# ScalarE takes its PSUM-emptying steps one tile place earlier in a transformer block on one core

## What is computed

```python
x = x + 0.5 * ffn(layernorm(x), Wq, Wk, Wv, Wo, Wff)
x = x + attn(layernorm(x), w_qkv, b_qkv, w_o, b_o)
x = x + 0.5 * ffn(layernorm(x), Wq, Wk, Wv, Wo, Wff)

def ffn(x):       # D = 256, 16 heads of 16
    scores = einsum('bqd,bkd->bkq', q, k) / sqrt(D)
    attn = softmax(scores, axis=-1)
    out = einsum('bkq,bkv->bqv', attn, v)
    z = l2_normalize(out @ Wo)
    z = l2_normalize(z @ Wff)
    return gelu(z)

def attn(x):      # 8 heads, no softmax
    return einsum('bhik,bhkj->bhij', einsum('bhik,bhjk->bhij', q, k), v) @ w_o.T + b_o
```

## Time and profile before

| what | value |
|---|---|
| median of 3 runs | 3134.5 us (3132.03 to 3140.0) |
| span of the profiled execution, first to last instruction | 3136.0 us |
| TensorE busy | 2897.9 us, 92% |
| VectorE busy | 2820.8 us, 90% |
| ScalarE busy | 2750.6 us, 88% |
| GpSimd busy | 896.6 us, 29% |
| mean granted TensorE clock | 0.975 of full speed |

### The profile page before, as it was taken

The page is one execution under the profiler, slowest core; times in us unless marked ns, Lnnn a source line. Parts: engine busy times, 40 slices in busy tenths (PEclk is TensorE's granted clock), DMA queues, the critical chain, the costliest instruction groups (busy, mean ns, idle before and its releaser), DMA issues.

```text
span 3136.0 us, 55848 instructions
## 1 busy us (share of the span) xinstructions
PE 2897.9 (92%) x15495; PEld 1082.9 (35%) x15784; DVE 2820.8 (90%) x5659; ACT 2750.6 (88%) x5028; POOL 896.6 (29%) x1195
## 2 busy tenths in 40 slices
PE   5999999999999999999999998999999999899997
PEld 2323343333333333334333332232323333232323
DVE  4999899998998989989989899899999999899996
ACT  3999888888888888888888889899898989999897
POOL 3323213323233132331333312232231222233131
PEclk8999999999999999999999999999999999999999
DMA  8222342223412333123321243323233332322332
GB/s 220 52 57 43 55 95 38 58 55 54 96 27 50 74 55 75 35 51 87 54 64 36 51 95 68 70 47 61 59 63 82 68 82 44 72 50 59 77 68 54
DMA packets 155198, 204.07 MB, mean 65 GB/s; under 512 B 34529, under 2 KB 88289, under 8 KB 154722
## 3 DMA queue, kind: packets, MB, share of 16 engines
q1 hardware_dynamic: 154594, 199.37, 30.4%
q0 software_dynamic: 256, 0.52, 0.1%
HBM read 46.66 MB, written 25.17 MB: 23 GB/s over the span
## 4 chain that ended last, share of the span: by engine, by line
PE 61%; issue 13%; DVE 11%; SPq 7%; ACT 4%; POOL 2%; DMA 1%; DVEq 0%; POOLq 0%; ACTq 0%
PE o_acc L840 20%; PE ring L826 19%; DVE exp_ring L655 9%; PE ring L870 7%; SPq L373 7%; PE ring L850 7%; PE ring L878 2%; PE ring L939 2%; PE ring L885 1%; ACT exp_ring L579 1%; ACT w_xn L591 1%; PE ring L862 1%; DMA kq_stack<-kq_parts 1%; PE ring L909 1%; PE ring L919 0%
## 5 line engine op out<-in xcount | busy, mean ns | idle before, releaser
L579 ACT ACTIVATE exp_ring<-exp_ring,neg_max 128x1024 f32<-128x1024 f32 x2048 | 2345.8, 1146 | 310.2 <-DVE exp_ring L655 295.1
L655 DVE TENSOR_SCALAR_CACHE_REDUCE exp_ring<-ring 128x1024 f32<-128x1024 f32 x2048 | 2413.6, 1216 | 208.7 <-PE ring L826 194.8
L826 PE MATMUL ring<-kq_stack 128*128 128x512 bf16 x3807 | 1064.3, 386 | 147.8 <-issue 57.1
L840 PE MATMUL o_acc<-exp_ring,v_scaled 128*32 128x512 f32 x8224 | 1114.2, 614 | 39.0 <-POOL v_scaled L512 23.2
L826 PEld LDWEIGHTS ring<-kq_stack 128*128 128x128 bf16 x4096 | 328.8, 98 | 1120.0 <-DVE exp_ring L655 418.7
L512 POOL TENSOR_TENSOR v_scaled<-v_now,exp_rsums 128x64 f32<-128x64 f32 x513 | 155.0, 302 | 1850.0 <-DVE exp_rsums L670 1830.4
L579 ACT ACTIVATION_READ_ACCUMULATOR exp_ring<-exp_ring,neg_max 128x1 f32 x2048 | 382.3, 187 | 0.0
L840 PEld LDWEIGHTS o_acc<-exp_ring,v_scaled 128*32 128x32 f32 x8224 | 163.0, 108 | 486.8 <-issue 416.3
L870 PE MATMUL ring<-xn_T,ffn_wqkv 128*128 128x512 f32 x528 | 271.4, 639 | 1.1 <-ACT xn_T L597 1.1
L850 PE MATMUL ring<-ffn_wo_wowff,o_T 128*128 128x256 f32 x1088 | 264.3, 387 | 2.0 <-DVE o_T L666 1.4
L850 PEld LDWEIGHTS ring<-ffn_wo_wowff,o_T 128*128 128x128 f32 x1088 | 199.5, 190 | 96.1 <-DVE exp_ring L655 54.3
(11 more groups left out here) (102 smaller groups left out, 1331.0 us busy)
## 6 DMA issues: line engine op xcount, KB each, us to landing
kq_stack<-kq_parts SPq DMA_DIRECT2D x2072, 64.0 KB, 2.4
x_post<-x_slots SPq DMA_DIRECT2D x17, 1024.0 KB, 5.5
x_prep<-x_slots SPq DMA_DIRECT2D x16, 1024.0 KB, 7.1
x_slots<-x_post SPq DMA_DIRECT2D x8, 1024.0 KB, 5.3
out<-x_post SPq DMA_DIRECT2D x8, 1024.0 KB, 4.6
x_prep<-in_L_attn_x SPq DMA_DIRECT2D x1, 1024.0 KB, 5.6
exp_ring<-in_L_attn_w_qkv SPq DMA_DIRECT2D x1, 512.0 KB
kq_stack<-kq_parts POOLq DMA_DIRECT2D x8, 64.0 KB, 3.7
```

Of the source, the lines that this page charges most:

```text
L579: nc.scalar.activation(e, e, ACT.Exp, bias=negmax[:, i % NM:i % NM + 1], scale=-1.0, accum_out=sums[:, g % EG, c:c + 1]).then_inc(exp_done, 1)
L655: nc.vector.tensor_scalar(E[:, (g % EG) * HQ + c, :].rearrange("p (b n) -> p b n", b=NB), ps, -1.0, None, ALU.mult, ALU.min, accum_out=neg ...
L826: last = mm(ps[:, n, :], kq[:, 0, c, j * P:(j + 1) * P], kq[:, 1, c, n * BANK:(n + 1) * BANK], start=True, stop=True)
L840: last = mm(O[32 * c:32 * c + 32, n, :], vsc[a][:, g % EG, c, :], E[:, (g % EG) * HQ + c, n * BANK:(n + 1) * BANK], start=(a == 0 and j == ...
```

## The change

Each engine now gets its own sorted list, from the same tables. On ScalarE's list the steps `qk`, `u`, `xt`, `xt2` and `gram` stand 1.0 place lower; `gelu`, `G`, `H` and the tiles stay. The lists of TensorE, VectorE and GpSimd, the slots, and SyncE's program are as before. All line numbers of the new kernel are one higher.

```diff
-    def section_steps(places, tiles, prep, post):
+    def section_steps(places, tiles, prep, post, lead):
         placed = []
 
         def put(place, *step):
-            placed.append((place % TILES, len(placed), step))
+            placed.append(((place - lead.get(step[0], 0)) % TILES, len(placed), step))
...
-    prologue = section_steps(PLAIN, False, True, False)
-    linear_body = section_steps(WITH_LINEAR, True, True, True)
-    plain_body = section_steps(PLAIN, True, True, True)
-    epilogue = section_steps(PLAIN, False, False, True)
+    LEAD = {"pe": {}, "act": {"qk": 1.0, "u": 1.0, "xt": 1.0, "xt2": 1.0, "gram": 1.0}, "dve": {}, "pool": {}}
+    prologue = {e: section_steps(PLAIN, False, True, False, LEAD[e]) for e in LEAD}
+    linear_body = {e: section_steps(WITH_LINEAR, True, True, True, LEAD[e]) for e in LEAD}
+    plain_body = {e: section_steps(PLAIN, True, True, True, LEAD[e]) for e in LEAD}
+    epilogue = {e: section_steps(PLAIN, False, False, True, LEAD[e]) for e in LEAD}
...
             def part(steps, p, linear):
-                slot, rank = slots_of(steps), ranks(steps)
-                for step in steps:
+                slot, rank = slots_of(steps), ranks(steps["act"])
+                for step in steps["act"]:
```

More of the change, by code:

```diff
@@ L315, in av_count @@
             return START + p * GROUPS + g + 3
-        LAST_SLOTS = [("last",) + s for s in linear_body if s[0] in PSUM_STEPS][-SLOTS:]
-        assert LAST_SLOTS == [("last",) + s for s in plain_body if s[0] in PSUM_STEPS][-SLOTS:]
-        assert LAST_SLOTS[0][1] == prologue[-1][0] == "v"
+        LAST_SLOTS = [("last",) + s for s in linear_body["pe"] if s[0] in PSUM_STEPS][-SLOTS:]
+        assert LAST_SLOTS == [("last",) + s for s in plain_body["pe"] if s[0] in PSUM_STEPS][-SLOTS:]
+        assert LAST_SLOTS[0][1] == prologue["pe"][-1][0] == "v"
         for steps in (prologue, linear_body, plain_body):
-            assert len([s for s in steps if s[0] in PSUM_STEPS]) % SLOTS == 0
+            assert len([s for s in steps["pe"] if s[0] in PSUM_STEPS]) % SLOTS == 0
         def slot_done(p, rank, step):
@@ L327, in slot_done @@
                 kind = step[1]
-                return before(p, kind) - PER[kind] + 1 + ranks(linear_body)[step[1:]]
+                return before(p, kind) - PER[kind] + 1 + ranks(linear_body["pe"])[step[1:]]
             return before(p, step[0]) + rank[step] + 1
@@ L333, in slots_of @@
             had = {} if steps is prologue else dict(enumerate(LAST_SLOTS))
-            for s in steps:
+            for s in steps["pe"]:
                 if s[0] in PSUM_STEPS:
@@ L475, in part @@
             def part(steps, p, linear):
-                rank = ranks(steps)
-                for step in steps:
+                rank = ranks(steps["pool"])
+                for step in steps["pool"]:
                     kind, i, r = step[0], index(step), rank[step]
@@ L642, in part @@
             def part(steps, p, linear):
-                slot, rank = slots_of(steps), ranks(steps)
-                for step in steps:
+                slot, rank = slots_of(steps), ranks(steps["dve"])
+                for step in steps["dve"]:
                     kind, i, r = step[0], index(step), rank[step]
@@ L807, in part @@
             def part(steps, p, linear):
-                slot, rank = slots_of(steps), ranks(steps)
-                for step in steps:
+                slot, rank = slots_of(steps), ranks(steps["pe"])
+                for step in steps["pe"]:
                     kind, i, r = step[0], index(step), rank[step]
```

## The result

The changed kernel takes 3119.1 us (median of 4 runs, 3117.3 to 3122.8) where the kernel before takes 3135.7 us (4 runs). The ratio is 0.9947, interval 0.9932 to 0.9961: 16.7 us less, where 17.9 were forecast. The sum was nearly right. Its parts were not, as the experiments show.

A forecast was written before the change was run, and what follows sets the result against it. The prediction took the order of waits, read from TensorE's, to bound the kernel, no engine's total alone. A 9.1 + B 6.2 + C 2.6 = 17.9 us off 3134.5 gave 3116.6 us, range 3103 to 3129.

The forecast's parts named there:

- A: Second `qk` step after the gelu, linear phases: copy and TensorE's restart 1.14 us earlier, in 8 phases 9.1 us.
- rival 3: A is taken back by VectorE's list or a DMA chain setting a later point: 3125.7 us, chance 0.08.
- The transposes: Two in each linear phase, TensorE waiting about 1 us each: their end costed at nothing, as VectorE is full there.
- B: Last `qk` copy of plain phases: the 1 MB load and TensorE's restart 1.03 us earlier at 6 loop ends, 6.2 us.
- Rival 2: At the plain loop ends the fetch does not follow the load, B is nothing: 3122.8 us, chance 0.15.
- C: `u` steps of the plain phases: TensorE's 16 waits on ScalarE's squares, 3.9 us, end; 2.6 us gained, bounds 0 and 3.9.
- D: First `qk` step after the gelu, plain phases: earlier copy costed at nothing, its gain waited out at `av` for `v_scaled`.
- Rivals 4 and 6: 4: TensorE's clock holds with less idle time, 3104 us, chance 0.10; 6: ScalarE becomes the chain, slower, rather 3145, chance 0.07.
- the prediction's first sign of being wrong: The prediction is wrong if, in the new profile, VectorE's reciprocals begin to wait for ScalarE.

The follow-up runs named there:

- e1: Kernel before with only ScalarE's copy of the second `qk` step of the linear phases one exp earlier: 3135.8 us, ratio 0.9999.
- e9: Kernel before with all the change's steps moved in the linear phases and none in the plain phases: 3135.0 us, ratio 0.9998.
- e5: Changed kernel with GpSimd's split of the linear phases' second `qk` step held until both `x1` operations are over: 3111.9 us, ratio 0.9919 to the kernel before.
- e11: e1 with GpSimd's split of that `qk` step held until both `x1` operations are over: 3130.5 us, ratio 0.9985 to the kernel before.
- e2: Kernel before with only ScalarE's copy of the last `qk` step of the plain phases one exp earlier: 3127.4 us, ratio 0.9975.
- e6: Kernel before with the plain phases' 1 MB load issued ahead of the first quarter's stack: 3115.1 us, ratio 0.9928.
- e3: Kernel before with only ScalarE's copy of the plain phases' first `qk` step after the gelu one exp earlier: 3136.9 us, ratio 1.0003.
- e4: Kernel before with all the change's moved steps except those of A, B and D: 3134.9 us, ratio 1.0002.
- e7: Changed kernel with the plain phases' 1 MB load issued ahead of the first quarter's stack: 3104.5 us, ratio 0.9895 to the kernel before.

## Why the prediction was right, and where not

*A, second `qk` step of the linear phases, 9.1 us: wrong.* TensorE's wait fell to 2.02 us, as forecast. The failed step is "So the chain runs through TensorE and 1.14 of VectorE's 1.49 us go", and the 8 by which it was multiplied. VectorE's idle time went whole, but 0.84 us of it went into the `x1` pair, since the same earlier copy starts GpSimd's split: the tile of 704.80 came 0.71 us earlier and not 1.14. And the phase of the earlier trace rows is one of the long ones. Over 48 such phases VectorE's idle time is 0.90 us on average and next to nothing in 13, so 0.06 us a phase was left, which e1's time cannot show. What VectorE won at 704.80 it did hand on, 0.65 of 0.71 us at `gram` (28.80 us from the tile in that phase of before, 28.15 in e1). The forecast followed the copy to TensorE and not to GpSimd, the other engine that waits for it, and it read one phase for eight. That is rival 3, A taken back, though by another cause than rival 3 names, and it had 0.08. Whole linear phases give 0 (e9).

*The transposes, nothing: not quite, in either kind of phase.* The premise was that VectorE is full behind 704.80 and covers them. But in e1 the stretch to `gram` is 28.15 us and TensorE still waits 0.99 and 1.18 us for ScalarE's copies in it; with the other steps moved too it is 27.83 in e9 and in the changed kernel, and 26.98 in e5 against 27.3 in e11. That is 0.3 us a phase, some 2.5 us in all, which e9's interval can hide. Which of the other moved steps does it was not tested. In the plain phases the 0.3 us waits (the other eight of the sixteen) stand in the part before the cut.

*B, 6.2 us: right in mechanism and nearly in size.* 8.1 us in e2, with 6.2 us less waiting; 7.3 us less waiting in the changed kernel. Rival 2 falls with e6: the stop does depend on how near the load is. That TensorE waits there for its code is still the prediction's reading: the rows name only "issue", and no run separates a fetch of code from another cause that the load delays.

*C, 2.6 us: undersized, and not independent.* The squares' waits fell from 3.9 us to nothing, so the upper bound was the value to take; with the transposes 0.6 to 1.1 us a phase is won by the table. It reaches the end only where D was moved as well.

*D, nothing: right alone, wrong in company.* e3 shows just the exchange that was forecast, 1.2 us at the copy and about 2.0 at `v_scaled`. But the prediction said that C's gain would "pass", without asking what D's place does to it: without D it is waited out there (e4).

*The sum.* Linear phases 0 for 9.1, plain phases 14.9 for 8.8. Two errors of opposite sign made 17.9 come close to 16.7. That was luck, and the total confirms neither part.

*Rivals 4 and 6.* Reciprocals wait for ScalarE 19.2 us in all instead of 13.7, so the prediction's first sign of being wrong shows a little, but ScalarE did not become the chain. The clock (below) holds more often: over its runs the changed kernel has a mean granted clock of 0.980, the one before 0.977. Rival 4's 3104 us did not come. A part of the plain phases' gain passes through it; how much is not separated.

## What to carry to other kernels

When a copy is moved forward, follow it to every engine that waits for it: TensorE restarted 1.14 us a phase earlier here, and GpSimd, released by the same copy, took 0.84 of it from VectorE. Before a wait is multiplied by the number of phases, read it in all of them: 1.49 us in the phase shown was 0.90 on average. Change the moved steps one by one and in groups: steps worth nothing alone added some 7 us together here, and a sum that comes out right proves none of its terms. Look for a stretch of fixed length up to the loop's end (here 110.35 us behind `gram`): ahead of it differences of a few tenths of a microsecond a phase can be read that no total time shows, if several executions of the same code are laid beside each other.

## What the runs showed of the hardware

*GpSimd and VectorE block each other.* Two `x1` additions of VectorE, 1.21 us each, take 2.35 us when GpSimd's split begins behind them (e5) and 3.19 us when it begins 0.14 us behind their start, and the split's first two operations then take 1.98 and 2.02 us instead of 1.04 and 1.16. The numbers fit turns: the first `x1` runs, the first operation (1.04 us) waits for it and then keeps the second `x1` waiting, which keeps the second operation waiting. In the kernel before, the split begins at 697.60, when the second `x1` has run for 0.14 us: the pair takes its 2.35 us, and the split's first operation takes 1.97. The Trainium skill, SBUF — State Buffer, section SBUF: two separate sides, says so: a VectorE operation with two inputs in SBUF and a GpSimd operation that reads SBUF take turns at a shared pair of ports, each holding it for its whole length. The traces of e1, e5 and the changed kernel agree.

*A loop's jump behind a large load.* In the changed kernel TensorE stops 4.2 to 4.7 us behind the issue of a 1 MB load and resumes 7.3 to 8.3 us behind it. In the kernel before it stops at 3.0 to 3.6 us and resumes at 7.6 to 8.2. Where the load is 9.2 us old at the stop (linear phases) the wait is 1.6 to 2.2 us, and where it is some 64 us old (e6) 1.8 to 2.3.

*The granted clock.* Windows of the kernel before and of e4 (stretch, length, busy us of PE, PEld, DVE, ACT and POOL, granted clock, DMA share, GB/s):

```profile
697.58:700.98 3.40, 3.40 (x12) 0.63 (x12) 3.40 (x6) 2.21 (x4) 3.23 (x3) 0.50 0.02 5
```

```profile
2302.50:2309.40 6.90, 5.12 (x16) 1.07 (x16) 4.34 (x10) 6.37 (x13) 4.05 (x4) 0.54 0.60 180
```

The first begins where a wait of TensorE of 3.16 us ends; the second begins inside such a wait, which ends at 2304.28. A granted clock of 0.50 is the lower level, 1.2 GHz instead of 2.4, and in the first window TensorE has it while it is busy for all of the 3.40 us. It also falls behind the shorter stops: 0.50 from 837.20 to 838.20, behind the 1.88 us of the loop end at 836.21. Over the whole execution TensorE is busy at the lower level for 115 us in the kernel before, 100 in the changed one, 72 in e7. The 13 short linear phases of the 48 are those in which the lower level lasts 3.4 us between the tile and `gram`, the 35 long ones those in which it lasts 6.8: with the second 3.4 us goes about 1 us more a phase. The executions of one kernel scatter with the clock: of the kernel before, the fastest beside e9 took 3129.8 us at a mean granted clock of 0.979 and the slowest 3141.6 us at 0.976. In e1 and in the changed kernel the stretch is 28.15 and 27.83 us at either length: no idle time of VectorE is left there ahead of the tile of 704.80.
